# Attention split three and five around the experts, the turn spread over four steps, and value products in quarters

## The reference

```python
xn = _layernorm(x, axis=-1)
# attention: 8 heads, 2 channels each for q and k, 16 for v
scores = jnp.einsum('bmhd,bnhd->bhmn', q, k) / math.sqrt(dqk)
scores = jnp.where(scores >= 0, scores, 0.2 * scores)
beta = jax.nn.softmax(scores, axis=-1)
out = jnp.einsum('bhmn,bnhd->bmhd', beta, v).reshape(B, M, C)
return gamma * out + x
# feed-forward: top 2 of 16 experts, capacity 1024 each; 12 are MLPs
dispatch = jnp.zeros((E, CAP, Hd), x.dtype).at[e_flat, slot].add(contrib)
h = jax.nn.gelu(jnp.einsum('ech,efh->ecf', dm, fc1_weight) + fc1_bias[:, None, :], approximate=False)
out_mlp = jnp.einsum('ecf,ehf->ech', h, fc2_weight) + fc2_bias[:, None, :]
gathered = expert_out[e_flat, slot]
```

## Time and profile before

| | us |
|---|---|
| median of 2 runs | 1056.45 (1056.41 to 1056.5) |
| the profiled execution | 1051.31 |
| its span on the core | 1049.5 |
| mean granted TensorE clock | 0.953 of 2.4 GHz |
| TensorE busy | 899.8 |
| VectorE busy | 776.2 |
| ScalarE busy | 694.1 |
| GpSimd busy | 578.6 |

### The profile page before, as it was taken

The page is one execution under the profiler, slowest core; times in us unless marked ns, Lnnn a source line. Parts: engine busy times, 40 slices in busy tenths (PEclk is TensorE's granted clock), DMA queues, the critical chain, the costliest instruction groups (busy, mean ns, idle before and its releaser), DMA issues.

```text
span 1049.5 us, 20085 instructions
## 1 busy us (share of the span) xinstructions
PE 899.8 (86%) x7619; PEld 367.1 (35%) x7620; DVE 776.2 (74%) x915; ACT 694.1 (66%) x803; POOL 578.6 (55%) x591
## 2 busy tenths in 40 slices
PE   0777612999999999999899999989999999999997
PEld 0444300222222222222377777752222222222222
DVE  6799986899998999899600000028999899989995
ACT  0566620778887878788754544447788877887885
POOL 2455523660373274076199998007754774774776
PEclk9987855899999999999999999999999999999999
DMA  8611100010010000001223323411102112102000
GB/s 217 246 47 46 46 13 24 29 41 2 26 43 16 17 32 22 13 15 33 68 71 125 105 86 121 126 52 28 32 12 68 28 28 61 28 18 58 13 28 25
DMA packets 48159, 55.29 MB, mean 53 GB/s; under 512 B 10714, under 2 KB 35122, under 8 KB 48080
## 3 DMA queue, kind: packets, MB, share of 16 engines
q1 hardware_dynamic: 39888, 44.84, 14.1%
q0 software_dynamic: 8192, 9.37, 3.0%
HBM read 31.57 MB, written 30.02 MB: 59 GB/s over the span
## 4 chain that ended last, share of the span: by engine, by line
PE 64%; DVE 13%; issue 8%; ACT 6%; POOL 5%; SPq 2%; DMA 1%; DVEq 1%; POOLq 0%; ACTq 0%
PE ps L732 19%; PE ps L712 12%; PE ps L702 11%; PE ps L790 8%; PE ps L782 8%; DVE ps L1002 6%; ACT pr L605 3%; POOL xs L444 2%; PE ps L656 2%; PE ps L742 2%; ACT ot L597 2%; PE ps L660 1%; POOL y L462 1%; SPq L248 1%; DVE xs L863 1%
## 5 line engine op out<-in xcount | busy, mean ns | idle before, releaser
L605 ACT ACTIVATE pr<-ps 128x1024 f32<-128x1024 f32 x512 | 523.2, 1024 | 164.9 <-PE ps L712 124.8
L1002 DVE TENSOR_SCALAR ps<-ps 128x1024 f32<-128x1024 f32 x512 | 601.2, 1225 | 13.8 <-PE ps L702 11.0
L732 PE MATMUL ps<-pr,vp 128*32 128x256 f32 x4096 | 328.5, 393 | 0.3
L712 PE MATMUL ps<-q,kz 64*128 64x512 bf16 x1024 | 201.8, 391 | 46.3 <-DVE ps L1002 46.2
L702 PE MATMUL ps<-q,kz 62*128 62x512 bf16 x1024 | 201.3, 390 | 12.3 <-ACT pr L605 8.4
L444 POOL DMA_INDIRECT xs<-eout,idxs x128 | 128.8, 1007 | 55.4 <-issue 32.8
L427 POOL DMA_INDIRECT disp<-xs,idxs x128 | 125.7, 982 | 46.5 <-issue 39.4
L712 PEld LDWEIGHTS ps<-q,kz 64*128 64x128 bf16 x1024 | 49.3, 93 | 263.9 <-DVE ps L1002 223.5
L1016 DVE TENSOR_TENSOR pr<-ps,parts 128x1024 f32<-128x1024 f32 x12 | 14.7, 1225 | 165.6 <-PE ps L790 165.6
L732 PEld LDWEIGHTS ps<-pr,vp 128*32 128x32 f32 x4096 | 81.4, 108 | 128.5 <-issue 126.2
L413 POOL TENSOR_TENSOR y<-y,att 128x256 f32<-128x256 f32 x32 | 23.1, 725 | 184.2 <-DVE att L990 178.6
(11 more groups left out here) (120 smaller groups left out, 655.7 us busy)
## 6 DMA issues: line engine op xcount, KB each, us to landing
disp<-pr SPq DMA_DIRECT2D x12, 512.0 KB, 5.0
eout<-pr SPq DMA_DIRECT2D x12, 512.0 KB, 3.0
y<-in_x SPq DMA_DIRECT2D x8, 512.0 KB, 7.2
out<-y SPq DMA_DIRECT2D x8, 512.0 KB, 3.3
w<-in_w1t SPq DMA_DIRECT2D x12, 256.0 KB, 3.2
w<-in_w2t SPq DMA_DIRECT2D x12, 256.0 KB, 3.4
xs<-disp SPq DMA_DIRECT2D x6, 512.0 KB, 5.2
pr<-disp SPq DMA_DIRECT2D x6, 512.0 KB, 4.9
```

Source lines behind the costliest of these rows:

```text
L605: act.activation(pr[:, c % BUFS, 2 * pair:2 * pair + 2, :], ring[i % RING], ACT.Exp, scale=SLOPE).then_inc(S["exps"], 1)
L712: last = pe.matmul(ring[i % RING][:, k, :], kz[r:r + TILE, hg, pair, kc * P:(kc + 1) * P], q2[r:r + TILE, hg, qh * HALF:(qh + 1) * HALF], ...
L732: last = pe.matmul(acc[p % 2][32 * g:32 * g + 32, cols], vp[:, hg, kc, g, :], pr[:, c % BUFS, g % PAIRS * 2 + g // PAIRS, cols], start=(kc ...
L1002: dve.tensor_scalar(s, s, 0.0, 1.0 / SLOPE - 1.0, ALU.max, ALU.mult).then_inc(S["relu"], 1)
```

## The change

`BH` becomes 3: three sequences of attention run ahead of the experts and five behind. The eight scatters now stand in three sequences (three, three, two) and the eight gathers in five (two, two, two, one, one). The transposes of the turn are issued one per step in steps 6 to 9, each between the scores and the second value product of its step. The value product of a step is cut into two quarters of 128 columns; the first stands between shifted and scores, the second where the whole stood. The reciprocal moves to unit 12, the scaling to unit 13, and it now stands ahead of that unit's rectification.

```diff
-BH = B // 2
+BH = 3
+SCATTERS = ((0, 1, 2), (3, 4, 5), (6, 7))
+GATHERS = ((0, 1), (2, 3), (4, 5), (6,), (7,))
...
-DENOM = 7
+DENOM = 12
+FINISH = 13
...
-            for k in range(1, BH):
+            for k in range(1, B - BH):
                 for hg in range(NHG):
                     load_operands(k + BH, hg)
-                for u in range(2):
-                    store_sequence(2 * k - 2 + u)
-            for u in range(2):
-                store_sequence(B - 2 + u)
+                for s in GATHERS[k - 1]:
+                    store_sequence(s)
+            for s in GATHERS[B - BH - 1]:
+                store_sequence(s)
...
-            def sequence(b, move, k, last):
+            def sequence(b, move, which, last):
 
                 value_rows(b, 1)
-                move(2 * k)
+                move(which[0])
                 add_attention(pass_at(b, 0, 0))
-                move(2 * k + 1)
+                for s in which[1:]:
+                    move(s)
                 if not last:
                     value_rows(b + 1, 0)
                 if move is gather:
 
-                    pool.wait_ge(S["comb"], CO0 + 2 * TB // GB * (k + 1))
+                    pool.wait_ge(S["comb"], CO0 + TB // GB * (which[-1] + 1))
...
-            def values(c, half):
+            def values(c, quarter):
...
-                cols = slice(half * HALF // 2, (half + 1) * HALF // 2)
+                cols = slice(quarter * P, (quarter + 1) * P)
...
-            def turn(p):
-                pe.wait_ge(S["acc_evac"], p + 1)
-                for t in range(GT):
-                    last = pe.transpose(acc[p % 2][:, t * P:(t + 1) * P], ot[:, p % 2, t * P:(t + 1) * P], ident)
-                last.then_inc(S["o_rdy"], 1)
+            def turn(p, t):
+                if t == 0:
+                    pe.wait_ge(S["acc_evac"], p + 1)
+                last = pe.transpose(acc[p % 2][:, t * P:(t + 1) * P], ot[:, p % 2, t * P:(t + 1) * P], ident)
+                if t == GT - 1:
+                    last.then_inc(S["o_rdy"], 1)
...
                 for i in range(first, end):
                     shifted(i)
+                    if i > first + PAIRS:
+                        values((i - 3) // PAIRS, (i - 3) % PAIRS * 2)
                     if i + AHEAD < end:
                         scores(i + AHEAD)
-                    if i % UP == TURN and i > first + UP:
-                        turn(i // UP - 1)
+                    if 0 <= i % UP - TURN < GT and i > first + UP:
+                        turn(i // UP - 1, i % UP - TURN)
                     if i > first + PAIRS:
-                        values((i - 3) // PAIRS, (i - 3) % PAIRS)
+                        values((i - 3) // PAIRS, (i - 3) % PAIRS * 2 + 1)
...
                     if done is not None and i % UP == DENOM:
                         denominators(done)
+                    if done is not None and i % UP == FINISH:
+                        finish(done)
                     dve.wait_ge(S["s1"], i + 1)
                     s = ring[i % RING]
                     dve.tensor_scalar(s, s, 0.0, 1.0 / SLOPE - 1.0, ALU.max, ALU.mult).then_inc(S["relu"], 1)
-                    if done is not None and i % UP == DENOM:
-                        finish(done)
```

More of the change, by code:

```diff
@@ L511, in _ @@
             for b in range(BH):
-                sequence(b, scatter, b, b == BH - 1)
+                sequence(b, scatter, SCATTERS[b], b == BH - 1)
             value_rows(BH, 0)
@@ L533, in _ @@
             pool.wait_ge(S["yo_out"], ONE + 16 * E_MLP)
-            for k in range(BH):
-                sequence(k + BH, gather, k, k == BH - 1)
+            for k in range(B - BH):
+                sequence(k + BH, gather, GATHERS[k], k == B - BH - 1)
         @block.scalar
@@ L606, in exponentials, with attention @@
                                ).then_inc(S["exps"], 1)
-            def attention(b0):
-                first, end = b0 * NUB, (b0 + BH) * NUB
+            def attention(b0, b1):
+                first, end = b0 * NUB, b1 * NUB
                 for i in range(first, end):
@@ L618, in attention @@
                 evacuate(end // UP - 1)
-            attention(0)
+            attention(0, BH)
             def take_turned(e):
@@ L642, in _ @@
                 expert(E_MLP - 2 + u, u, u == 1)
-            attention(BH)
+            attention(BH, B)
         @block.tensor
@@ L715, in shifted @@
                 last.then_inc(S["s2"], 1)
-            def values(c, half):
+            def values(c, quarter):
                 p, kc = divmod(c, TB)
                 hg = p // NQ % NHG
-                cols = slice(half * HALF // 2, (half + 1) * HALF // 2)
+                cols = slice(quarter * P, (quarter + 1) * P)
                 pe.wait_ge(S["exps"], PAIRS * (c + 1))
-                if kc == 0 and half == 0:
+                if kc == 0 and quarter == 0:
                     if p == 0:
@@ L733, in values, with attention @@
                                      pr[:, c % BUFS, g % PAIRS * 2 + g // PAIRS, cols],
-                                     start=(kc == 0 and half == 0), stop=(kc == TB - 1), tile_position=(0, 32 * g),
+                                     start=(kc == 0 and quarter == 0), stop=(kc == TB - 1), tile_position=(0, 32 * g),
                                      skip_group_check=True)
-                if half:
+                if quarter == 3:
                     last.then_inc(S["pv"], 1)
-            def turn(p):
-                pe.wait_ge(S["acc_evac"], p + 1)
-                for t in range(GT):
-                    last = pe.transpose(acc[p % 2][:, t * P:(t + 1) * P], ot[:, p % 2, t * P:(t + 1) * P], ident)
-                last.then_inc(S["o_rdy"], 1)
-            def attention(b0):
-                first, end = b0 * NUB, (b0 + BH) * NUB
+            def turn(p, t):
[4 more added lines that the diff above has]
+                    last.then_inc(S["o_rdy"], 1)
+            def attention(b0, b1):
+                first, end = b0 * NUB, b1 * NUB
                 for i in range(first, first + AHEAD):
@@ L750, in attention @@
                     shifted(i)
+                    if i > first + PAIRS:
+                        values((i - 3) // PAIRS, (i - 3) % PAIRS * 2)
                     if i + AHEAD < end:
                         scores(i + AHEAD)
-                    if i % UP == TURN and i > first + UP:
-                        turn(i // UP - 1)
+                    if 0 <= i % UP - TURN < GT and i > first + UP:
+                        turn(i // UP - 1, i % UP - TURN)
                     if i > first + PAIRS:
-                        values((i - 3) // PAIRS, (i - 3) % PAIRS)
+                        values((i - 3) // PAIRS, (i - 3) % PAIRS * 2 + 1)
                 for j in range(end - 3, end):
-                    values(j // PAIRS, j % PAIRS)
-                turn(end // UP - 1)
-            attention(0)
+                    for k in range(2):
+                        values(j // PAIRS, j % PAIRS * 2 + k)
+                for t in range(GT):
+                    turn(end // UP - 1, t)
+            attention(0, BH)
             def turn_rows(e, u):
```

## The result

| | before | after |
|---|---|---|
| median, us | 1056.45 (2 runs) | 1109.96 (2 runs, 1108.74 to 1111.18) |
| ratio | | 1.051, 95% interval 1.046 to 1.056 |
| profiled execution, us | 1051.31 | 1108.74 |
| its span, us | 1049.5 | 1106.9 |
| first rectification starts at | 172.1 | 177.2 |

The change made the kernel 5.1% slower. The predicted 1099 us was 11 us short of it; the range (1070 to 1136) holds it. The 5.1 us by which the first rectification comes later belong to the prologue, whose code is the same in both; the profiled execution of before was itself 5.1 us under its two timed runs. Attention and experts together grew by 919.3 - 866.9 = 52.4 us, which is the 53.5 us of the medians but for 1.

The account below looks back on a forecast made before the run. Attention is bound by a 1.20 us ring, TensorE needing 1.11. Units rise to 1.35 us, transposes add 0.80 a pass: 22.4 for 21.1, 30 passes at +1.3 plus first passes, +43 on 1056.45, giving 1099 us, range 1070 to 1136.

Parts of the forecast that it names:

- The ring: Attention, two units: scores, values, shifted, exponential, then scores reusing its slot; 2.40 us, so 1.20 a unit.
- the 1.9 us a pass: At the turn: a pass of 21.1 us exceeds 16 units of 1.20; this stall was what the change could remove.
- The gap: TensorE in attention: about 0.10 us at each change of matmul form, four per unit in the new order for two.
- The rival without a gap: Weights loaded ahead remove the gap, VectorE sets the unit at 1.15 us; -46, 1010 us; chance 0.05.
- the half-priced one: The added changes of form cost about half, 1.22 to 1.25 us a unit; -16, 1040 us; chance 0.06.
- the cancelling one: At 1.27 to 1.29 us a unit, new cost and removed stall nearly cancel; 1056 us (1045 to 1070); chance 0.07.
- the dear one: Quarters dearer: 1.42 us a unit, pass 23.5, +77, 1133 us; chance 0.10.
- The rival in which GpSimd binds: Scatters or gathers take some 10 us more than computed, 5 to 6 us in three sequences; 1116 us; chance 0.07.
- A quarter is half: Value products: a quarter's two groups stream 0.11 us each, half of 0.22; with the gap a quarter takes 0.355.
- The turn in four steps: TensorE's transposes, one per step, cost 0.20 us each, 0.80 us a pass.
- Hidden work: In the new unit TensorE never waits, so the longer unit is not hidden; ring, VectorE and ScalarE come loose.
- GpSimd: Three scatters or two gathers plus value rows end 3.5 and 5.0 us before TensorE wants them; no cost.

Follow-up runs that it names:

- moving the product: Kernel before with the whole value product moved between shifted and scores; ratio to before 1.045 (1.039 to 1.051).
- The later read alone: Kernel before with VectorE's reciprocal moved from unit 7 to 9 and its scaling to unit 10; 1242.38 us for 1270.29, ratio 0.979.
- side-by-side quarters: Changed kernel with both value quarters of 128 columns behind the scores; 1303.74 us for 1271.42, ratio 1.025, undisturbed passes 20.05 us.
- the whole rearrangement with whole products: Changed kernel with the value product whole again, 256 columns once per step behind the scores; 1241.02 us for 1271.42, ratio 0.976.

## Why the prediction was right, point by point

**What bounds the kernel.** Right. The ring at 1.20 us a unit, with TensorE at 1.11 behind it, was confirmed from both sides: one more pair of changes made TensorE the bound at 1.355, and moving the product made another ring the bound at 1.305, both within 0.01 us of what the rows of before give. One reading was too wide: the 1.9 us a pass is not all stall. The later read alone gives back 1.07, and the rest stays with the turn. The prediction charges the new pass 0.80 for its transposes, so its sum is not hurt.

**The gap.** The forecast stood on this step: 0.10 us each time the form of the matmul changes, twice more per unit. After shows 0.32, 0.36, 0.32 and 0.36 for the four intervals that were put at 0.32, 0.355, 0.315 and 0.355. By the whole unit the two added changes cost 1.355 - 1.11 = 0.245 us, 0.12 each: the gap and the 0.02 to 0.03 that a first group takes beyond its stream, as the prediction had it. The side-by-side quarters show that it is the change of form and not the width or number of records. The rival without a gap (1010 us), the half-priced one (1040), the cancelling one (1056) and the dear one (1133) all fall with the unit. The rival in which GpSimd binds (1116) is near the measured 1110, but it is not what happened: TensorE never waited for value rows (below).

**A quarter is half.** Right: its second group starts 0.13 us after the first, and the next shifted comes 0.22 to 0.23 after that, 0.11 of stream and 0.11 of gap as before.

**The turn in four steps.** This term was mis-sized: 0.26 us a transpose, not 0.20. I took what the last of four transposes takes up to the values. One alone is also the first of its form, and the first of four in the trace of before was followed after 0.165 us, the next two after 0.11. 4 x 0.06 is 0.24 us a pass, 7 of the 9.4 us by which the sum for attention was short (52.4 for 43). The rest is the unit, 1.355 for 1.35 (0.08 a pass, 2.5 us).

**Hidden work.** VectorE idles 93.5 us over 512 rectifications, 0.18 each, as forecast; ScalarE 0.33 before an exponential; no wait before the reciprocal but at the ends of the two stages.

**GpSimd.** Right on the first chip, with less to spare than computed for the scatters. Timelines of GpSimd in the kernel after, from the add that closes sequence 0 to the value rows of sequence 2, which TensorE wants at 372.65:

```profile
294.71 0.73 POOL L416 TENSOR_TENSOR y<-y,att 128x256 f32<-128x256 f32 x1 [18.23 <-DVE att L999]
...
369.61 0.66 POOL L409 COPY vp<-va 128x544 f32<-128x544 f32 x1 [1.52 <-DMA disp<-xs,idxs]
```

The copy ends at 369.61 + 0.66 = 370.27. 370.27 - 294.71 = 75.6 us for the 74.0 computed, and 2.4 us of slack for 3.5. For the gathers the copy ends at 825.74 and is wanted at 831.19: 5.4 for 5.0.

**Three and five** costs nothing, as computed; that it brings nothing was seen alone too (ratio 0.998). The stall could have been removed without it.

**Where the gain of the later reads went.** It was real: 1.0 to 1.1 us a pass (21.07 to 20.0), some 34 us over 32 passes. It was taken back by the quarters, 2.7 us a pass, some 86. Both are passes of the second chip, between its pauses; their difference, some 52 us, agrees with the 52.4 of the first.

## What to carry to other kernels

Before splitting matmuls to fill a wait, count the changes of form (tile shape of the array) per turn of the loop: here two more of them cost 0.245 us a unit, where the unit had 0.09 to spare. When an engine stalls on another's result, look first at where in its own queue it asks: moving VectorE's read two units later won as much as the whole rearrangement with whole products. A unit that no engine fills is held by a ring, a loop of waits that closes on itself; write down all rings before moving anything, those too that run partly through waits and partly through one engine's own order over several steps, since an order that opens one ring can close another.

## What the runs showed of the hardware that I had not expected

On the chip of the experiments, ScalarE and VectorE, and with them TensorE, stand still for 5 to 10 us at a time, and up to 14.6 in one run, while GpSimd issues indirect DMAs, and TensorE's granted clock falls to 0.50 in these pauses; the kernel before takes 1260 to 1271 us there for 1056 on the first chip, and 1123 without its scatters. A matmul stream of doubled, narrower records costs TensorE nothing between the pauses (20.05 us a pass in both) and yet 63 us in the whole kernel there, 1304 for 1241. And one fp32 transpose of 128 columns between matmuls of other forms takes 0.26 us of TensorE's queue, where four in a row take 0.58 to 0.59.
